# Output projection of the last two batches during token choice, and minima of the scores one pair ahead

## The reference, cut to what matters

```python
h = _ln(x1) + shift;  q, k, v = split(h @ Wqkv.T)          # 16 heads of 64
attn = softmax(_ln(q) @ _ln(k).T / 8);  o = attn @ v
x2 = x1 + o @ Wout.T                                        # output projection
gate = softmax(x2 @ Wgate.T)                                # 8 experts
vals, idx = top_k(gate.T, 512)                              # each expert chooses 512 of the 4096 tokens
g = _ln(x2[idx]);  y = (gelu(g @ fc1.T + b1) @ fc2.T + b2) * vals
out = x2 with y added at idx
```

## Time and profile before

| | |
|---|---|
| median of 3 runs | 1431.27 us |
| profiled execution | 1431.61 us |
| its span, first to last instruction | 1429.8 us |
| TensorE matmul busy | 1370.5 us, 96% |
| ScalarE, VectorE, GpSimd busy | 1035.9, 960.7, 911.5 us |
| mean granted TensorE clock | 0.987 of full speed |
| first scores of batch 0 | at 365.3 us |
| first scores of batch 15 / last | 1117.0 / 1151.4 us |
| token choice begins / ends | 1167.1 / 1205.5 us |
| first expert's first product | 1225.7 us |

### The profile page before, as it was taken

How to read it: one execution, slowest core, us unless ns; L and a number is a source line. 1 busy time by engine, 2 the same in 40 slices (tenths; PEclk the granted TensorE clock), 3 DMA queues, 4 the chain that set the end, 5 groups by cost and what they waited for, 6 DMA issues and landing times. The chain is left out here.

```text
span 1429.8 us, 30429 instructions
## 1 busy us (share of the span) xinstructions
PE 1370.5 (96%) x10795; PEld 1183.3 (83%) x10795; DVE 960.7 (67%) x2191; ACT 1035.9 (72%) x2703; POOL 911.5 (64%) x855
## 2 busy tenths in 40 slices
PE   7899999997899999999999999999999988999996
PEld 6799999996678887888888788788888777889896
DVE  5876667643776676677667667666755568678763
ACT  5556666565898889889888988988988732476662
POOL 2576666652678768867877876786787620354643
PEclk9899999999999999999999999999999999999999
DMA  5342222111100100110110011011011046145522
GB/s 159 114 129 67 68 67 68 49 45 30 38 9 30 53 23 31 53 45 9 52 46 31 30 53 36 18 53 45 9 45 46 30 148 253 45 104 156 137 35 30
DMA packets 61638, 89.04 MB, mean 62 GB/s; under 512 B 6144, under 2 KB 50992, under 8 KB 58800
## 3 DMA queue, kind: packets, MB, share of 16 engines
q1 hardware_dynamic: 53232, 75.82, 16.3%
q0 software_dynamic: 6144, 8.39, 3.6%
q10 hardware_dynamic: 2112, 2.88, 0.6%
HBM read 61.90 MB, written 25.18 MB: 61 GB/s over the span
## 5 line engine op out<-in xcount | busy, mean ns | idle before, releaser
L1386 POOL TENSOR_TENSOR prob<-prob,share_p 128x512 f32<-128x512 f32 x256 | 271.6, 1067 | 195.6 <-DVE share_p L1493 195.0
L1487 DVE TENSOR_REDUCE shift<-bank 128x2 f32<-128x512 f32 x256 | 164.7, 685 | 186.0 <-PE bank L1103 185.9
L1258 ACT ACTIVATE prob<-bank,shift 128x256 f32<-128x256 f32 x512 | 237.8, 479 | 64.3 <-DVE shift L1487 64.2
L147 PE MATMUL bank<-wqkv_h,rowsT_h 128*128 128x512 f32 x384 | 158.9, 414 | 2.8 <-PEq L311 1.7
L147 PE MATMUL bank<-wqkv_h,rowsT_l 128*128 128x512 f32 x384 | 151.5, 395 | 0.0
L147 PE MATMUL bank<-wqkv_l,rowsT_h 128*128 128x512 f32 x384 | 150.8, 393 | 0.0
L1115 PE MATMUL bank<-ident,prob 128*128 128x128 f32 x1024 | 142.7, 281 | 1.1 <-POOL prob L1386 1.1
L1374 POOL TENSOR_TENSOR landing<-landing,rq 128x512 f32<-128x512 f32 x128 | 131.1, 1046 | 8.4 <-DVE rq L1441 8.4
L1130 PE MATMUL bank<-pT,landing 128*64 128x256 f32 x1024 | 127.1, 388 | 1.7 <-ACT pT L1345 1.7
L1115 PEld LDWEIGHTS bank<-ident,prob 128*128 128x128 f32 x1024 | 109.5, 141 | 21.3 <-POOL prob L1386 3.7
L1258 ACT ACTIVATION_READ_ACCUMULATOR prob<-bank,shift 128x1 f32 x512 | 107.5, 210 | 0.0
(11 more groups left out here) (324 smaller groups left out, 4517.6 us busy)
## 6 DMA issues: line engine op xcount, KB each, us to landing
landing<-in_fc1s SPq DMA_DIRECT2D x6, 1024.0 KB
landing<-in_fc2s SPq DMA_DIRECT2D x6, 1024.0 KB
rows<-in_x SPq DMA_DIRECT2D x16, 256.0 KB, 2.9
xT<-in_xT SPq DMA_DIRECT2D x16, 256.0 KB, 2.7
x_again<-in_x SPq DMA_DIRECT2D x16, 256.0 KB, 2.8
x_rows<-x SPq DMA_DIRECT2D x16, 256.0 KB, 3.1
rows<-x_rows SPq DMA_DIRECT2D x16, 256.0 KB, 3.1
x<-x_rows SPq DMA_DIRECT2D x16, 256.0 KB, 2.9
```

Source lines behind the costliest of these rows:

```text
L147: last = nc.tensor.matmul(out, a, b, start=(n == 0), stop=(n == 3 * len(ks) - 1))
L1258: last = nc.scalar.activation(prob[at][:, n, :], score_bank[side][:, n * T:(n + 1) * T], ACT.Exp, bias=shift[:, at, n:n + 1], scale=-1.0, ...
L1386: nc.gpsimd.tensor_tensor(prob[at][:, :, :], prob[at][:, :, :], share[:, at, :].unsqueeze(2).to_broadcast([P, TT, T]), ALU.mult).then_inc( ...
L1487: nc.vector.tensor_reduce(shift[:, s % 2 * 2 + side, :], score_bank[side][:, :].rearrange("p (n m) -> p n m", n=TT), AX, ALU.min).then_inc ...
```

## The change

1. Batches 14 and 15 (the "late" ones) are no longer projected in the attention. Their logits are made without x2: at the start of the attention (t = -1, s = 2) 16 small products give Wc = Wout.T Wgate.T for each pair, VectorE splits it, and `logits_of` multiplies it with o of the late batch: 16 products of 256 columns for a batch, against 48 for a projection. A copy (`from_o`) and two small products add it to x1 @ Wgate.T in the router's matmuls. The transposes of x1 and the router's matmuls of batches 14 and 15 stand at s = 4, 5, 6 of the last batch, and in `finish`.
2. The projection of both is done in the block of token choice (`late_step`), batch 15 first: its first eight steps stand where six idle products stood ahead of the transposes of the gates, two steps follow each of the digits 0 to 11 in place of idle products. ScalarE and GpSimd take sums, squares and roots there and write x2 and normalised rows. SP stores o of batch 14 to HBM during batch 15 and reads it back.
3. In batch 15 the scores of odd pairs go to the two chunk banks, those of even pairs to the score banks; scores(s) waits for the exponentials of pair s-2 instead of s-1. VectorE takes the minima of pair s+1 in pair s, the first before `invert(t, s, 1)`, the second behind it.
4. Smaller: values of the last pairs use one half of a bank, so values(q) waits for o_lo of all pairs before q; x1 of batch 1 is loaded at the end of the first block; the raw piece of the experts' weights shares a tile with its low part; tiles and semaphores are reused to make room.

The core of the diff:

```diff
 def scores(t, s, odd):
+    if closing(t) and s == 1:
+        wait(pe, chunk_out, 12, t, 12)
+        wait(pe, out_proj, TT, t - 2, TT)
+    elif closing(t) and s > 1:
+        wait(pe, exped, H, t, 2 * s - 2)
+    else:
+        wait(pe, exped, H, t, 2 * s)
@@ VectorE, step(t), for s
-    if live(t):
+    if live(t) and (not closing(t) or s == 0):
         lowest_of(t, s, 0)
         lowest_of(t, s, 1)
     ... (low part of o, invert(t, s, 0), copy of the transposed half of pair s-1)
+    if closing(t) and s + 1 < PAIRS:
+        lowest_of(t, s + 1, 0)
     ...
     invert(t, s, 1)
+    if closing(t) and s + 1 < PAIRS:
+        lowest_of(t, s + 1, 1)
@@ TensorE, step and finish
-        if closing(t) and s in PROJ_PAIRS:
-            project(t - 1, PROJ_PAIRS.index(s), 1 - odd)
-        if closing(t) and s >= 4:
-            for k in range(0 if s == 4 else s - 3, s - 2):
-                project_last(k, odd)
         if closing(t):
+            if s == LATE_PAIR[True]:                 # 3
+                logits_of(t - 1, 0, 1 - odd)
+                logits_of(t - 1, 1, 1 - odd)
             fill(t, 2 * s + 1)
 def finish(t, its):
-    fill(t, 1)
     values(t - 1, PAIRS - 2, its)
     transposes(t - 1, PAIRS - 1)
-    project_last(PAIRS - 3, its)
+    logits_of(t - 1, 0, its)
+    values(t - 1, PAIRS - 1, its)
+    logits_of(t - 1, 1, its)
     fill(t, 3)
-    values(t - 1, PAIRS - 1, its)
-    project_last(PAIRS - 2, its)
-    project_last(PAIRS - 1, its)
@@ experts, SP
+    for arrived, n in zip(stored, (16 * LATE_FROM, 16 * LATE_FROM, 32 * NB)):
+        sp.wait_ge(arrived, n)
+    sp.wait_ge(o_stored, O_STORED + 128 * (LATE - 1))
     for t, src in (... the five tables ...):
         sp.dma_start(t, src).then_inc(loaded, 16)
+    for i, b in enumerate(LATE_ORDER):               # 15, 14
+        sp.dma_start(late_x[i][:, :, :], x1_rows[bass.ds(b * T, T), :]...).then_inc(late_in[i], 16)
+        if i > 0:
+            load_late_o(i)
+    load_halves(sp, w1_in, (w1_h, w1_l), halves[0:2], 0)
@@ experts, TensorE
-    idle_products(6)
+    def late_step(i, k):
+        ...
+        if k == HW // P - 1 and i == 0:
+            pe.wait_ge(late_in[0], 16 + 16)
+        ...
+        for m, (o, w) in enumerate(((high, wo_h), (high, wo_l), (low, wo_h))):
+            nc.tensor.matmul(late_bank(i), o[:, k, rows], w[:, k, :], start=(k == 0 and m == 0), stop=False)
+        if k == HW // P - 1:
+            nc.tensor.matmul(late_bank(i), ident[:, :], late_x[j][:, i % TT, :], start=False, stop=True).then_inc(late_made, 1)
+    for k in range(HW // P):
+        late_step(0, k)
     pe.wait_ge(gated, 1)
     ... (transposes of the gates; the digits)
@@ experts, ScalarE
     nc.scalar.activation(gates[:, :, :], gates[:, :, :], ACT.Exp).then_inc(exped, 1)
+    take(0)                                          # copy with sum, waits for late_made
+    spread_of(0)                                     # mean, then squares with sum
     for n in range(DIGITS):
```

More of the change, by code:

```diff
@@ L152 @@
 EARLY = 2
+LATE = 2
+LATE_FROM = NB - LATE
+O_STORED, LATE_STORED, WC_IN = 16 * 7, 32, 80
+LATE_ORDER = [NB - 1] + list(range(LATE_FROM, NB - 1))
 def build(nc, a, out):
@@ L926, in fill_at, with attention @@
             slot += 1
-        if slot == i:
+        if slot == i and not (name in ("x2", "gates") and t + TR_LAG[name] >= NB - 2):
             return t + TR_LAG[name], name, j
     return -1, None, 0
-def attention(nc, exponent, weights, rows_of, banks, ident, x1_rows, hbias, cols, x2_rows, logit, out, a, halves, sbuf, sems):
+def attention(nc, exponent, weights, rows_of, banks, ident, x1_rows, hbias, cols, x2_rows, logit, out, a, halves, out_weights, o_kept, o_stored,
+              spent, sbuf, sems):
+    wo_h, wo_l, o_h, o_l, _ = out_weights
+    wc_in, wc_made, wc_done = spent
     landing, o_raw, wgate, wo_hi, wo_lo, (x2_stored, x2n_stored, ew_stored) = weights
@@ L1091, in _, with logit_weights @@
             def _(pe):
+                def logit_weights():
+                    pe.wait_ge(wc_in, WC_IN + 64)
+                    for m in range(PAIRS):
+                        for k in range(KT):
+                            last = nc.tensor.matmul(score_bank[0][:, m * E:(m + 1) * E], prob[m // 2][:, k, m % 2 * P:(m % 2 + 1) * P], wgate[:, k, :],
+                                                    start=(k == 0), stop=(k == KT - 1))
+                    last.then_inc(wc_made, 1)
                 def scores(t, s, odd):
+                    if first(t) and s == 0:
+                        pe.wait_ge(wc_done, NB + 2)
                     if s == 0:
@@ L1472, in out_norm @@
                             nc.vector.tensor_scalar(out_var[:, :], out_moment[:, :, 1], LN_EPS, None, ALU.add).then_inc(out_spread, 1)
-                    if s == (1 if closing(t - 1) else OUT_APPLY_PAIR) and live(t - 2) and part < TT:
+                    if s == OUT_APPLY_PAIR and live(t - 2) and not is_late(t - 2) and part < TT:
                         wait(dve, out_root, 1, t - 2, 1)
@@ L1558, in _, with experts @@
                 steps(step)
-def experts(nc, a, landing, halves, banks, ident, cols, x2_rows, logit, out, stored, sbuf, sems):
+LATE_STEPS = [2] * 12 + [0] * 3
+TAKEN_IN, SPREAD_IN, NORMED_IN = {4: 1, 8: 2, 12: 3}, {5: 1, 9: 2, 13: 3}, {1: 0, 7: 1, 11: 2}
+def experts(nc, a, exponent, landing, halves, banks, ident, cols, x1_rows, x2_rows, logit, out, stored, out_weights, o_kept, o_stored,
+            spent, sbuf, sems):
+    late_stored, late_made, late_taken, late_centred, late_squared, late_normed, late_rooted, late_links, *late_in = spent
+    wo_h, wo_l, o_h, o_l, kept = out_weights
     s = ExitStack()
@@ L1968, in step @@
                         wait_e(pool, tr_done, KT, later - 1, KT)
+                        if first(later):
+                            pool.wait_ge(last_rows, 16 * (LATE_FROM + 1))
                         hold()
```

331 lines of the change are left out of this document (226 added, 105 removed).

## The result

| | before | after |
|---|---|---|
| median of runs | 1431.18 us (4) | 1445.14 us (4; 1441.07 to 1449.27) |
| profiled execution / span | 1431.61 / 1429.8 | 1445.87 / 1444.1 |
| granted clock, mean | 0.987 | 0.977 |

What follows compares the result with a forecast made beforehand. TensorE, busy 96% of the span, was taken as the bound. Terms 4.4 - 1.7 + 3.6 + 0.3 + 0.7 + 1.0 = +8.3 us on 1431.27 gave 1439.6 us, range 1432 to 1445.5.

Steps and rivals of the forecast that it cites:

- (c): Batch 15's pairs: the clock falls in most of them, +5 to +7 us over the +1.0, 1444 to 1447; chance 0.10.
- (d): Choice: its stores or loads come late and hold the gather, +5 us, 1445; chance 0.04.
- The closing pairs: Batch 15, scores(1) to scores(7): six loops of 4.5 us plus 5.6 of other TensorE work, +4.4 us.
- Rival (a): Batch 15's pairs: second reciprocal never held, pairs at TensorE's 2.95 us, -4.9 instead of +4.4, total 1429.3; chance 0.10.
- The end of the attention: Scores(7) of batch 15 to the next block's first product: 14.7 us against 16.4, -1.7 us.
- The start of the choice: First late row block waits for x1, gate transposes begin at 6.3 us instead of 3.1: +3.6 us, bounds +2.4 and +4.3.
- the term for the issue of x1: Start of choice: x1 issued sixth, 2.3 us behind the block's start, landing 3.1 later, at 5.4.
- The digits: Token choice: six late products replace six idle ones per digit and fit its idle time; 0 to +1.2, taken +0.3 us.
- The start of the attention: Late weights' products ahead of q's transposes, 3.9 us, partly hidden; bounds -1.0 and +3.9, taken +0.7 us.
- The clock: Batch 15's pairs: gaps of 1.55 us may halve TensorE's clock; bounds 0 and +8, one stretch taken, +1.0 us.

Runs made afterwards that it cites:

- the fastest run: Changed kernel plus minima behind o_l, x1 first, three idle products per digit, late weights' products in halves, last two pairs' values in free score banks: 1427.56 us, ratio 0.9978.

## Why the forecast was right in sign and short by 6 us

The measured 1445.14 us is 5.5 above the forecast, and the spans differ by 6.0 from it. It is inside the range of 1432 to 1445.5 by 0.4 us only, above the 1435 to 1443 that the chances gave the forecast itself, and where rivals (c) and (d) had their times, by neither of their mechanisms.

- **The closing pairs: the loop right, the sum partly by luck.** The loop was 4.55 us where the steps gave 4.49, at the place named, and two runs show it: with the order mended it goes, with the gap filled it stays. Rival (a) fell at its own point; with o_l and the reciprocals ahead of the next pair's minima, the plain pair runs at 2.94 us, where (a) had 2.95. Scores(0) to (7) grew by 5.95 against 4.4 + 1.0, but two errors offset each other in that. The prediction took scores(1) for untouched by the change. It came 3.97 us behind scores(0) instead of 5.54, since the stretch at half clock that pair 0 had before did not come again (eight products of the values took 1.08 us instead of 1.98); why is open. The row from before:
```profile
1119.68 1.98 PE L1130 MATMUL bank<-pT,landing 128*64 128x256 f32 x8
```
From scores(1) to (7) the growth was 7.52 us against 5.4. Pair 3 took 8.72, not 4.49 + 2.0. TensorE waited 2.03 us for GpSimd's probabilities there, 0.65 more than in pair 2, because VectorE has two instructions that normalise rows of x2 between the minimum and the reciprocal, a term that the sum lacks:
```profile
1135.94 0.73 DVE L1553 TENSOR_SCALAR x2n<-x,out_moment,out_rstd 128x256 f32<-128x256 f32 x2
1136.58 0.16 DVE L1570 RECIPROCAL share_p<-denom 128x2 f32<-128x2 f32 x1
```
Then the clock was at half, worth 1.56 us by the run with the gap filled. Of the rest, 0.3 is the loop's 0.06 six times and 0.4 is in pair 4, which waits 0.32 us for o_l.
- **The end of the attention, right:** -1.83 against -1.7.
- **The start of the choice, 1 us short.** The mechanism was right, as the run with x1 first shows, and the term for the issue of x1 wrong: I carried over 2.3 us for five issues from the earlier trace rows, they took 3.71, and TensorE went on at 6.67 instead of 5.4.
- **The digits, the term that was off by most.** The prediction set +0.3, for half clock as something that might add 0.1 us to a digit. Measured: +3.04, at a clock of 0.61. The 0.1 was right for the plain digits at half clock (1.98 to 2.01 us instead of 1.90). What it lacked is 0.3 to 0.5 us in each of three digits, two in which a row block ends and the one behind the first of them, and 1.27 us in the digit with six idle products, behind which the next sum waits. Six idle products are 12 passes of 128 columns and took 1.58 us at full clock; the six late ones in their place took 0.96. With three idle ones more and x1 first the clock is 1.00 and the stretch 29.06: +0.36. The term was right for full clock; what I priced too low was its loss, and even that price varies between executions, from +1.2 to +3.05 us with the same instructions.
- **The start of the attention, 1.2 us short, and 1.7 us not foreseen.** +0.7 stood below the middle of wide bounds (-1.0 and +3.9); the steps alone (+1.6) would have been nearer to +1.94. Another 1.70 us lie between scores(0) of batch 0 and of batch 15. Of these 1.23 are in batch 0's first step (46.10 us against 44.87), where the clock was 0.79 from 383 to 391 us against 1.00. Seven of the 13 profiled kernels with the late logits have this dip (0.79 to 0.82) and take 46.10 to 46.37 us for the step; the six with the clock at 1.00 take 44.86 to 44.88, as the kernel before does. So the dip is worth 1.2 to 1.5 us, and some executions don't have it; of the kernel before there is one profile. The other 0.47 us are spread over the fourteen steps behind it, 0.03 to 0.05 us in each; in the other runs they come to 0.5 to 1.1 us in sum. Why these steps are longer is open.
- **The clock.** I set one +1.0 for it, in the closing batch. A stretch at half clock was there, 1.56 us in pair 3, but the kernel before had one that cost as much in pair 0 and is gone: in the closing batch the clock cost nothing on balance. Its cost fell elsewhere, 2.7 us in the digits and 1.2 in batch 0's first step. Rival (c) had the place wrong: the plain closing pairs ran at full clock. The rule in the Trainium skill, "TensorE: Matmul & The Clock Gate", section "A second HAM failure mode: psum-queue depth-cycling", would have had the whole closing batch swing between the levels; this trace shows one low stretch in it, in pair 3.
- **Late stores, rival (d).** Not in the changed kernel. In the fastest run the end of the choice waits 2.50 us for a store, below.

The forecast took the clock as a penalty on gaps in the closing batch only. By the spans 6.0 us were missing (14.3 against 8.3): 2.7 in the digits, 1.7 from scores(0) of batch 0 to batch 15, 1.2 at the start of the attention, 1.0 at the start of the choice, 0.5 in the closing pairs, and -1.2 in the rest, of which 0.7 behind the choice.

## What to carry to other kernels

On an engine with a fixed order, work put ahead of its time is a wait put ahead of what is ready: before moving an instruction forward, list what stands behind it (here a reciprocal and o_l) and who waits for that. A second set of banks wins nothing if it is taken from another loop of the same length. When real products take the place of idle ones, read the granted clock of the stretch before and after: here six real ones took 0.96 us where six idle ones had taken 1.58, the clock went to 0.61, and that cost ten times the term that I had for it; three idle ones beside them held it at 1.00.

## What I had not expected of the hardware

The clock fell twice at the start of the choice, and it was full in between. In the changed kernel, window by window (columns as for the digits):
```profile
1176.00:1178.00 2.00, 2.00 (x12) 2.00 (x11) 1.41 (x6) 0.28 (x1) 0.00 (x0) 0.50 0.36 117
1179.00:1182.00 3.00, 0.78 (x5) 0.75 (x6) 0.00 (x0) 0.00 (x0) 0.00 (x0) 1.00 0.83 232
1182.50:1184.50 2.00, 0.04 (x1) 0.00 (x0) 1.78 (x8) 1.58 (x7) 0.67 (x2) 0.50 1.10 352
```
Ahead of the block TensorE had waited 0.94, 0.56 and 0.53 us; then it ran 21 products without a gap, with the clock at half from the second microsecond on (4.06 us, where 0.12 each would be 2.5). It was back at 1.00 while TensorE waited 2.61 us for x1, and at half again when the digits began. So an engine that waits can show the full clock, and what the wait costs is seen only behind it. Without that wait (x1 first) the first digits ran at 1.00 and the later ones fell to 0.50; with a wait of 0.87 us (one set of banks) the first digit ran at 1.00 and the clock fell in the second. In the runs that load x1 first and have three idle products in each digit, the first 15 products were slow too (3.44 us in the first of them), and the clock was at 1.00 in all the digits. Which of the gaps makes it fall isn't shown.

In the fastest run the block of the choice ends late. TensorE stands ahead of the next block,
```profile
1204.66 2.92 PE L1686 MATMUL bank<-ident 128*128 128x128 f32 x24 [2.50 <-PEq L1742]
```
and SP's waits (line, what for, total, times, longest) name a store of late rows:
```profile
SPq L1742 <- DMA out<-late_x: 4.9, 1, 4.9
```
Its 256 KB took 9.2 us from issue to landing, behind two loads of 1 MB (weights and a bias) issued in the 2 us ahead of it on the same queue. The Trainium skill, "DMA: Bandwidth & Descriptors", section "Queues, rings and completion order", says that each DMA engine takes up one ring's descriptors in the order in which they were put there; the long landing agrees. Issuing these stores ahead of the loads would be worth up to 2.2 us more as an estimate (2.50 against 0.30 before the change); this was not run.
